# Low parts of ten projection weights made by GpSimd instead of VectorE, in the first two token blocks of an attention and expert kernel

## The reference

```
xn   = layernorm(x)
q, v = xn @ Wq, xn @ Wv
state[t] = sigmoid(beta) * state[t-1] + v[t]        # along the sequence, 16 heads
y    = layernorm(q * state) * ln_g + ln_b
y    = y * silu(xn @ Wg)
attn = y @ Wo
ffn  = sum over the top 8 of 64 experts of
       weight * ((silu(xn @ w1) * (xn @ v1)) @ w2)  # an expert takes at most 128 tokens
out  = x + attn + ffn
```

## Time and profile before

| what | value |
|---|---|
| median of 3 runs | 2477.35 us (2476.07 to 2477.9) |
| the profiled execution, its own time | 2477.67 us |
| its span, first to last instruction | 2476.0 us |
| granted TensorE clock, mean | 0.994 |
| PE busy | 2421.0 us (98%) |
| DVE busy | 1625.2 us (66%) |
| ACT busy | 1307.5 us (53%) |
| POOL busy | 675.8 us (27%) |

### The profile page before, as it was taken

The page is one execution under the profiler, slowest core; times in us unless marked ns, Lnnn a source line. Parts: engine busy times, 40 slices in busy tenths (PEclk is TensorE's granted clock), DMA queues, the critical chain, the costliest instruction groups (busy, mean ns, idle before and its releaser), DMA issues.

```text
span 2476.0 us, 35288 instructions
## 1 busy us (share of the span) xinstructions
PE 2421.0 (98%) x12113; PEld 2098.4 (85%) x12113; DVE 1625.2 (66%) x1689; ACT 1307.5 (53%) x1435; POOL 675.8 (27%) x523
## 2 busy tenths in 40 slices
PE   7999999999999999999999999999999999999997
PEld 6888778888888888888888888888888888888886
DVE  7776798766666665666566666657666666656653
ACT  5557323654556654566445565455655456544653
POOL 3221122223323232322223222332233222323321
PEclk9999999999999999999999999999999999999998
DMA  7796855797668966779676797766986679867685
GB/s 276 262 315 198 254 188 200 252 300 235 197 222 277 309 222 215 234 252 298 239 234 211 256 308 248 236 217 224 316 273 197 227 234 292 271 216 234 221 273 158
DMA packets 143621, 606.10 MB, mean 245 GB/s; under 512 B 20592, under 2 KB 20656, under 8 KB 143024
## 3 DMA queue, kind: packets, MB, share of 16 engines
q1 hardware_dynamic: 116304, 518.91, 59.0%
q0 software_dynamic: 27232, 86.00, 16.2%
HBM read 520.89 MB, written 100.70 MB: 251 GB/s over the span
## 4 chain that ended last, share of the span: by engine, by line
PE 81%; DVE 9%; DMA 4%; ACT 4%; issue 2%; SPq 0%; POOL 0%; ACTq 0%; DVEq 0%; POOLq 0%
PE psA L1564 16%; PE psA L1565 16%; PE psA L1566 16%; PE psH L1564 5%; PE psH L1566 5%; PE psH L1565 5%; PE psY L1564 3%; PE psY L1566 3%; PE psY L1565 3%; DVE ew_lo L1169 3%; ACT ew_hi L770 3%; DMA ew_raw<-ew_dram 2%; PE psX L1677 2%; PE psY L1596 2%; DVE pw_lo L1164 1%
## 5 line engine op out<-in xcount | busy, mean ns | idle before, releaser
L1169 DVE TENSOR_TENSOR ew_lo<-ew_raw,ew_hi 128x1536 fp32r<-128x1536 f32 x384 | 694.0, 1816 | 331.4 <-ACT ew_hi L770 324.1
L770 ACT ACTIVATE ew_hi<-ew_raw 128x1536 fp32r<-128x1536 f32 x384 | 568.3, 1483 | 138.4 <-DMA ew_raw<-ew_dram 72.2
L1564 PE MATMUL psA<-xT_hi,pw_hi 128*128 128x512 f32 (+1 forms) x1544 | 612.1, 396 | 10.2 <-DVE pw_lo L1164 4.0
L1565 PE MATMUL psA<-xT_lo,pw_hi 128*128 128x512 f32 (+1 forms) x1544 | 603.7, 391 | 0.0
L1566 PE MATMUL psA<-xT_hi,pw_lo 128*128 128x512 f32 (+1 forms) x1544 | 603.5, 391 | 0.0
L764 ACT ACTIVATE pw_hi<-pw_raw 128x1024 fp32r<-128x1024 f32 x254 | 266.5, 1058 | 615.7 <-PE psA L1566 585.2
L1164 DVE TENSOR_TENSOR pw_lo<-pw_raw,pw_hi 128x1024 fp32r<-128x1024 f32 x256 | 317.5, 1247 | 128.9 <-ACT pw_hi L764 123.4
L1564 PEld LDWEIGHTS psA<-xT_hi,pw_hi 128*128 128x128 f32 x1544 | 292.2, 189 | 69.6 <-issue 13.2
L1564 PE MATMUL psH<-ew_hi,gT_hi 128*128 128x384 f32 x1024 | 346.4, 338 | 4.2 <-DVE ew_lo L1169 4.2
L1566 PEld LDWEIGHTS psA<-xT_hi,pw_lo 128*128 128x128 f32 x1544 | 291.9, 189 | 62.0
L1566 PE MATMUL psH<-ew_hi,gT_lo 128*128 128x384 f32 x1024 | 343.6, 336 | 0.0
(11 more groups left out here) (168 smaller groups left out, 3154.7 us busy)
## 6 DMA issues: line engine op xcount, KB each, us to landing
ew_raw<-ew_dram SPq DMA_DIRECT2D x384, 768.0 KB, 6.3
pw_raw<-proj_w_dram SPq DMA_DIRECT2D x256, 512.0 KB, 5.0
xn_scratch<-xt SPq DMA_DIRECT2D x33, 512.0 KB, 4.8
xt<-x_dram SPq DMA_DIRECT2D x32, 512.0 KB, 5.9
out_dram<-x_dram SPq DMA_DIRECT2D x32, 512.0 KB, 5.8
out_dram<-ot POOLq DMA_DIRECT2D x32, 512.0 KB, 8.9
xn<-xn_turned SPq DMA_DIRECT2D x29, 512.0 KB, 4.3
xn_turned<-xraw SPq DMA_DIRECT2D x28, 512.0 KB, 5.3
```

What stands on the lines that cost most here:

```text
L770: act.activation(ew_hi[:, c % 3, :], ew_raw[:, c % 3, :], ACT.Copy).then_inc(s_ewhi, 1)
L1169: dve.tensor_tensor(ew_lo[:, c % 3, :], ew_raw[:, c % 3, :], ew_hi[:, c % 3, :].bitcast(F32), ALU.subtract).then_inc(s_ewlo, 1)
L1564: pe.matmul(dst, l_hi, r_hi_, start=first, stop=False)
L1565: pe.matmul(dst, l_hi, r_lo_, start=False, stop=False)
```

## The change

GpSimd gets a function `weights_lo` that does the same subtraction as `proj_lo`. It makes two low parts in block 0's output stage (the weights `n2(0, 2, 0)` and `n2(0, 2, 1)`, right behind the write of pass 0) and eight in block 1's value and query stage (all weights of slot 0, each ahead of an `add_sums`). VectorE drops these ten and keeps the others. Because `s_pwlo` counts in order, each side waits for the other's last one.

```diff
@@ gpsimd
+            def weights_lo(n, slot, hi, lo):
+                pool.wait_ge(s_pwhi, n + 1)
+                pool.wait_ge(s_pwlo, n)
+                pool.tensor_tensor(lo[:, slot, :, :], pw_raw[:, slot, :, :], hi[:, slot, :, :].bitcast(F32),
+                                   ALU.subtract).then_inc(s_pwlo, 1)
...
                 add_out(0, mm)
+                if mm == 0:
+                    for w in range(2):
+                        weights_lo(n2(0, 2, w), w, *out_room(2))
...
                 for h in range(2):
+                    weights_lo(n1(1, mm, 2 + 2 * h), 0, pw_hi, pw_lo)
                     add_sums(1, mm, h)
@@ vector
-                if mm < 3:
+                if mm in (0, 2):
                     for w in range(2):
-                        proj_lo(n2(0, (1, 2, 4)[mm], w), w, out_room((1, 2, 1)[mm]))
+                        proj_lo(n2(0, mm + 1 if mm == 0 else 4, w), w, out_room(1))
...
                 elif mm == 1:
+                    dve.wait_ge(s_pwlo, n2(0, 3, 0))
                     for w in range(2):
                         proj_lo(n2(0, 3, w), w, out_room(3))
...
                 scan(1, mm, 0)
-                proj_lo(n1(1, mm, 2), 0)
                 list8(done)
                 times_q(1, mm, 0)
+                dve.wait_ge(s_pwlo, n1(1, mm, 3))
                 proj_lo(n1(1, mm, 3), 1)
                 list8(done + 1)
                 scan(1, mm, 1)
-                proj_lo(n1(1, mm, 4), 0)
                 if ROUNDS_VQ[mm] > 2:
                     list8(done + 2)
                 times_q(1, mm, 1)
+                dve.wait_ge(s_pwlo, n1(1, mm, 5))
                 proj_lo(n1(1, mm, 5), 1)
```

## The result

| kernel | median, us | runs | range, us |
|---|---|---|---|
| before | 2478.34 | 15 | 2475.00 to 2483.55 |
| changed | 2473.45 | 15 | 2470.76 to 2476.79 |

The ratio is 0.9981, with a 95% interval of 0.9974 to 0.9987: 4.9 us less. It was measured again later: 12 runs of the changed kernel gave a median of 2477.19 against 2478.49 in 23 of the kernel before, a ratio of 0.9991 (0.9981 to 1.0001). All 27 runs of the changed kernel have a median of 2475.16, and all 98 timed beside the experiments or the result for the kernel before 2478.08. So the gain is best put at 3 us (a ratio of 0.9988, inside the second interval and at the edge of the first), and the first measurement was on the large side. The profiled execution took 2470.76 us over a span of 2469.1.

The account below looks back on a forecast made before the run. PE holds 81% of the chain, but waits in block 1's value and query stage, where VectorE has no room. 2477.67 - 4.4 + 0.5 - 1.7 = 2472.1, less 0.3 for the median: 2471.8 us, range 2468.8 to 2477.0.

Parts of the forecast that it names:

- Part 1: Block 1's value and query stage: eight low parts leave VectorE, PE becomes the bound, row sums start earlier; -4.4 us.
- the walk from the first scan to the single stall of 0.7: Block 1's stage head: VectorE starts 2.3 us late, PE stalls once, 0.7 us plus some 0.2 restart, near 329 us.
- The rule that I went by: SBUF lock between GpSimd and VectorE instructions with two SBUF inputs; VectorE's one-input list rounds stay free.
- Part 2: GpSimd's low parts in block 1: 2.6 us each, hidden by the running query projection; price 0.
- The limit of 4.1 us: Block 1, slot 0: a GpSimd low part may take 4.1 us before PE waits.
- Part 3: Block 0's output stage: two low parts on GpSimd, second load starts 3.2 to 4.4 us later; chain moves +0.5 us.
- The rival in which the output stage takes the gain back: Block 0's output stage: 8.08 us transfer stays, chain 3.2 to 4.4 us later; 2475.1, or 2476.8 with low clock; chance 0.20.
- Part 4: Behind block 1's row sums: the gap goes and the low clock of 3.5 us with it; -1.7 us.
- GpSimd too slow: Block 1's slot 0 and block 0's pair: subtraction takes 5 us beside VectorE, PE waits at eight weights; 2485, chance 0.07.
- no effect: Whole kernel: the time won is lost again at a later wait of PE; 2477.3, chance 0.04.
- The clock stays as it was: Low clock falls behind block 1's row sums again or at another short idle time; 2473.5, chance 0.24.

## Why the prediction was right, and where it was not

The forecast of 2471.8 us lies 1.7 under the median of 2473.45, inside the range, and the gain was foreseen at 5.5 us against 4.9 in the first measurement and 3 over all. That the first measurement came so close is in part luck, since over all runs the gain is little more than half of the forecast. The mechanism held; two of its terms, the stage and the clock, were too big.

**Part 1, VectorE freed.** Shown, by the half with the eight alone. The term was -4.4 us. With the low clock at the head in both, the stage shortened by 3.2 (100.10 to 96.90), 1.2 less than the term. The other two profiles of the kernel before, without that low clock, have 98.96 and 98.94; the changed kernel's would be 1.6 shorter without it (what the low stretch takes from a stage that PE bounds: 94.19 less 92.57), so 95.3, which is 3.6 less. The step that failed is the walk from the first scan to the single stall of 0.7: it took `start` at its length of before. It took 1.95, the scan began at 311.01, 11.2 us behind PE's start where it had been 9.5, and two weights were late by 0.84 each. Moving one round away removed both stalls, moving `start` removed all of them but 0.27 us, and that brought another 2.7 and 2.2 us, which shows it. The rest went as foreseen: from 353 us on VectorE idles for 1.54 us ahead of every second scan. The rule that I went by was too narrow: VectorE's held-up low part at 355.86 has two inputs in SBUF, and I let everything with one input off. The rounds, which are most of VectorE's work, were indeed not touched (the MATCH_REPLACE8 at 321.10 took 2.28 us with GpSimd's subtraction beside it from 321.15); `start` was. The Trainium skill (SBUF — State Buffer, "SBUF: two separate sides") names for the lock also VectorE instructions in a 2-port mode, and says that whichever starts first keeps the port for its whole instruction. The prediction had taken from that page only the case of two inputs. `start` ending with GpSimd's instruction, and not before, agrees with the second half; which mode it runs in, no run here shows.

**Part 2, GpSimd's price.** The subtraction took 2.40 us in the median against 2.6. The limit of 4.1 us was borne out by the kernel that makes each twice: 4.8 us, seven waits, 7.2 us. The price of 0 was right for GpSimd's own time and wrong in what it did to `start`.

**Part 3, the pair in block 0.** The chain was said to move by +0.5 us. From the first output matmul to block 1's first one it took 51.36 and 51.56 us in the changed kernel's two profiles, and 51.65, 50.73 and 50.82 in the three of the kernel before: 0.3 less by the first pair of profiles, 0.4 more by the means, with a scatter of 0.9 between profiles of one kernel. So +0.5 can't be told from nothing. The kernel with this pair alone has 50.43 and no change in time. The pair took 6.23 us with VectorE's split between, and the second load could be issued from 275.1 on, both as foreseen. What I left open was the length of that load, and it came near the short end: the load that took 8.08 us still lands at 279.6, so nearly all of its delay is taken off its length. The rival in which the output stage takes the gain back is out; when the delay is doubled it comes true, with 3.1 us.

**Part 4, the clock.** In this execution it went as said: 1.00 behind the row sums. As a term of the median it was too large. The low stretch stood behind the gap in two of four executions, so the gap's removal is worth half of 1.7 us, some 0.8, if these four are typical. And the low stretches wander through the whole kernel from one run to the next. The timed runs show no such gain: the mean granted clock is 0.9937 over 83 runs of the kernel before and 0.9938 over 27 of the changed one, a difference worth 0.2 us, with a standard error of 0.5.

**The sum by what was measured.** At equal clock the clock's term is taken out, and two are left: -3.6 for the stage and, by the means of the profiles, +0.4 for the output stage, together -3.2. The runs give -2.9 at equal clock (2477.6 to 2474.7), with a standard error of 0.3, so nothing of size is missing. The clock's term comes on top as 0 to -0.8. The medians as they stand differ by 2.9 over all runs and by 4.9 and 1.3 in the two measurements: the clock of the single runs scatters them.

**The rivals.** GpSimd too slow (2485) is excluded by the rows above, and so is no effect (2477.3), by the stage of 96.90 and 96.91 us, though the interval of the second measurement alone reaches it. The clock stays as it was (2473.5) is half right. That its time is the one that came in the first measurement is chance: in the profiled execution the clock was full behind the row sums, and the term that missed was the stage's.

## What to carry to other kernels

Work that leaves a full engine is worth what the next bound leaves, here PE's 5.46 us a projection. The first weights after the move have no slack at all, so walk through the hand-over row by row and not only through the steady state. Before you give GpSimd an elementwise operation, list what VectorE runs at that moment, small instructions too, since one of eight columns can wait as long as GpSimd's whole instruction; then put the two engines' work at different times. Find the time after which the receiver waits, here 4.1 us, since each instruction beyond it costs its excess again.

## What the runs showed of the hardware that was not expected

- A VectorE product of 128x8 elements with one tensor input took 0.23 us alone and 1.89 to 2.84 us beside a GpSimd subtraction of 128x1024 (eight profiles), ending with it each time; MAX8 and MATCH_REPLACE8 over 2048 elements kept 2.27 to 2.29 us beside it.
- GpSimd took 2.40 us for a subtraction that takes VectorE 1.21, and 6.23 for two (268.91 to 271.80 and 271.94 to 275.14) with a VectorE split of two inputs from 270.36 to 272.89, which itself took 2.53 instead of 1.22.
- The mean granted clock of a run lies between 0.990 and 0.996, and each 0.001 goes with 2.0 us; the low stretches, mostly of some 3.5 us at 0.51 to 0.58, change their place from one execution to the next. A term that rests on one of them in one profile counts for less than its length.
- A low stretch at the head of block 1's stage cost 1.1 us where VectorE bounds it (100.10 against 98.95) and 1.6 where PE does (94.19 against 92.57), for the same 1.7 us of lost clock.
